# A Perceiver block on one core: the probabilities are turned by a DMA block exchange and VectorE's 32x32 transposes in place of TensorE's transposes

## What is computed

```python
def _L0_xattn_ref(query, key):            # query (1, 256, 2048), key (1, 25088, 2048)
    a = jnp.einsum('bqd,bkd->bqk', query, key)
    e = jax.nn.softmax(a, axis=-1)
    c = jnp.einsum('bqk,bkd->bqd', e, key)
    return c
...
    x = x + _L0_xattn_ref(_layernorm(x, axis=-1), ctx_4096)
    x = x + _L0_attn_ref(_layernorm(x, axis=-1), L0_attn_Wq, L0_attn_bq, L0_attn_Wk, L0_attn_bk, L0_attn_Wv, L0_attn_bv)
    x = x + _L0_ffn_ref(_layernorm(x, axis=-1), L0_ffn_W_base, L0_ffn_b_base, L0_ffn_W_gate, L0_ffn_A, L0_ffn_B)
```

## Time and profile before

| | us |
|---|---|
| median of 3 runs | 2488.42 |
| lowest and highest of them | 2483.71, 2494.42 |
| the profiled execution | 2496.61 |
| its span, from first to last instruction | 2494.9 |
| PE busy in it | 2443.1 (98%) |
| DVE, ACT and POOL busy | 1963.5 (79%), 1098.1 (44%), 1416.6 (57%) |
| mean clock granted to TensorE | 0.995 of full |

### The profile page before, as it was taken

How to read it: one execution, slowest core, us unless ns; L and a number is a source line. 1 busy time by engine, 2 the same in 40 slices (tenths; PEclk the granted TensorE clock), 3 DMA queues, 4 the chain that set the end, 5 groups by cost and what they waited for, 6 DMA issues and landing times.

```text
span 2494.9 us, 36102 instructions
## 1 busy us (share of the span) xinstructions
PE 2443.1 (98%) x11446; PEld 2011.2 (81%) x11446; DVE 1963.5 (79%) x2702; ACT 1098.1 (44%) x1577; POOL 1416.6 (57%) x1056
## 2 busy tenths in 40 slices
PE   6999999999999999999999999999999999999799
PEld 5888888888888888888888888888888888868577
DVE  8888888888878888888888888888878888674356
ACT  4444444444444444444444444444444444443443
POOL 2766666666666555566565565555656656552341
PEclk9999999999999999999999999999999999999899
DMA  9988888788888988888988888888898888878533
GB/s 237 255 213 229 219 207 231 207 232 217 205 231 217 224 216 217 211 220 204 230 215 201 220 218 218 216 212 220 206 228 210 208 218 218 214 158 156 130 121 100
DMA packets 421367, 518.22 MB, mean 208 GB/s; under 512 B 54470, under 2 KB 296134, under 8 KB 418504
## 3 DMA queue, kind: packets, MB, share of 16 engines
q1 hardware_dynamic: 411336, 475.66, 78.1%
q0 software_dynamic: 9984, 41.95, 5.1%
HBM read 488.71 MB, written 28.84 MB: 207 GB/s over the span
## 4 chain that ended last, share of the span: by engine, by line
PE 93%; SPq 3%; DMA 2%; DVE 1%; ACT 0%; issue 0%; ACTq 0%; DVEq 0%
PE ps L1457 30%; PE ps L1459 30%; PE ps L1458 30%; PE ps L1466 2%; SPq L439 1%; DMA q_t<-qk_dram 1%; SPq L567 1%; DMA quart<-in_ctx_dram 1%; PE ps L1686 0%; PE ps L1632 0%; PE ps L1759 0%; PE ps L1485 0%; DVE acc L1203 0%; DMA qk_dram<-q_nat 0%; SPq L432 0%
## 5 line engine op out<-in xcount | busy, mean ns | idle before, releaser
L618 POOL TENSOR_TENSOR nat_lo<-raw,nat_hi 128x512 fp32r<-128x512 f32 x784 | 1171.0, 1523 | 862.3 <-ACT nat_hi L778 830.2
L1082 DVE TENSOR_TENSOR ch_lo<-tr,ch_hi 128x512 fp32r<-128x512 f32 x784 | 762.2, 972 | 296.9 <-ACT ch_hi L767 293.2
L767 ACT CAST ch_hi<-tr 128x512 fp32r<-128x512 f32 x784 | 481.1, 621 | 796.9 <-PE ps L1459 776.9
L1457 PE MATMUL ps<-ch_hi,xt_hi 128*128 128x512 f32 x1696 | 673.1, 397 | 9.9 <-DVE ch_lo L1082 6.4
L1459 PE MATMUL ps<-ch_hi,xt_lo 128*128 128x512 f32 x1696 | 662.9, 391 | 0.0
L1458 PE MATMUL ps<-ch_lo,xt_hi 128*128 128x512 f32 x1696 | 662.2, 390 | 0.0
L1457 PE MATMUL ps<-nat_hi,pt_hi 128*128 128x512 f32 x1568 | 610.3, 389 | 1.6 <-DVE pt_lo L1023 1.6
L1459 PE MATMUL ps<-nat_hi,pt_lo 128*128 128x512 f32 x1568 | 610.3, 389 | 0.0
L1458 PE MATMUL ps<-nat_lo,pt_hi 128*128 128x512 f32 x1568 | 610.0, 389 | 0.0
L1078 DVE STREAM_TRANSPOSE tr<-quart 128x512 f32<-128x512 f32 x784 | 547.6, 699 | 2.1 <-DMA quart<-in_ctx_dram 2.1
L778 ACT CAST nat_hi<-raw 128x2048 fp32r<-128x2048 f32 x196 | 374.4, 1910 | 206.7 <-PE ps L1459 184.0
(11 more groups left out here) (200 smaller groups left out, 1397.8 us busy)
## 6 DMA issues: line engine op xcount, KB each, us to landing
quart<-in_ctx_dram SPq DMA_DIRECT2D x392, 512.0 KB, 8.4
raw<-in_ctx_dram SPq DMA_DIRECT2D x196, 1024.0 KB, 8.2
wq_in<-in_L_attn_Wq_dram POOLq DMA_DIRECT2D x16, 1024.0 KB, 6.4
win<-in_L_ffn_W_base_dram SPq DMA_DIRECT2D x64, 256.0 KB, 6.8
tr<-wt_dram POOLq DMA_DIRECT2D x64, 256.0 KB, 3.2
wt_dram<-stage SPq DMA_DIRECT2D x32, 256.0 KB, 5.5
wt_dram<-stage_b SPq DMA_DIRECT2D x32, 256.0 KB, 10.3
wq_dram<-wq_out POOLq DMA_DIRECT2D x16, 256.0 KB, 2.3
```

The source lines that it names most:

```text
L618: last = pool.tensor_tensor(nat_lo[:, j, t], raw[:, j % 2, t], nat_hi[:, j, t].bitcast(F32), ALU.subtract)
L767: act.copy(ch_hi[:, c % RING_CH, :], tr[:, c % RING_TR, :]).then_inc(chunk_hi, 1)
L1082: dve.tensor_tensor(ch_lo[:, c % RING_CH, :], tr[:, c % RING_TR, :], ch_hi[:, c % RING_CH, :].bitcast(F32), ALU.subtract).then_inc(chunk_s ...
L1457: pe.matmul(out_, a_hi, b_hi, start=start, stop=False)
```

## The change

The probabilities no longer go through TensorE, in the 47 turns for which `by_dma` holds (turns 2 to 48: not the first, not the second, not the end). Instead

- ACT writes `probs` with the keys of a tile in another order (the 32-key groups that belong to one partition quarter side by side),
- SP copies the four 128-column blocks of a query tile to the four partition quarters of a new tile `quads`, four DMAs of 64 KB for each tile (runs of 512 bytes), 8 for a turn, ahead of the next loads,
- DVE turns `quads` by 32x32 blocks back into `probs` (two instructions of 128x512 for a turn, `turn_probs`, which write every fourth element),
- `pt_hi` and `pt_lo` are then made out of `probs` in SBUF, not out of PSUM.

Pieces 0 and 1 of the sum stand one chunk later on PE, with them the first `nat_hi` piece on ACT and the first two updates of `acc` on DVE. On DVE the transposition of chunk c+3 now stands behind the work on the probabilities. `quads` takes the room of `b_nat`, so all 8 experts' loads stand in the last turn.

```diff
+        quads = put(at_b, "quads", [P, TT, QR, P])
...
+                self.by_dma = not (self.first or self.second or self.over)
...
-        PIECE_AFTER = {5: 0, 7: 1, 9: 2, 11: 3, 13: 4, 15: 5}
+        PIECE_AFTER = {6: 0, 8: 1, 9: 2, 11: 3, 13: 4, 15: 5}
...
+            def move_probs(turn, q):
+
+                sp.wait_ge(probs_ready, turn.times(TT, q + 1 - TT))
+                for b in range(QR):
+                    sp.dma_start(quads[b * SQ:(b + 1) * SQ, q], probs[:, q, b * P:(b + 1) * P]).then_inc(probs_moved[q], 16)
+
             def next_block(turn, m=None):
 
                 step = turn.step if m is not None else None
+                if turn.by_dma:
+                    for q in range(TT):
+                        move_probs(turn, q)
...
             next_block(REST[0], LAST_M)
-            for e in range(EXPERTS // 2):
-                load_expert(e)
...
+            for q in range(TT):
+                move_probs(REST[1], q)
             sp.wait_ge(chunk_transposed, DC * (NB - 1) + CH)
...
             sp.dma_start(x_nat[:], x_dram).then_inc(x_again, 16)
-            for e in range(EXPERTS // 2, EXPERTS):
+            sp.wait_ge(lo_drained, G_PT + TT * (NB - 1))
+            for e in range(EXPERTS):
                 load_expert(e)
...
             def softmax(turn, q):
...
-                act.activation(probs[:, q, :], ps[:, SCORE_BANK + TT * new + q, :], ACT.Exp,
+                to, of = probs[:, q, :], ps[:, SCORE_BANK + TT * new + q, :]
+                if turn.by_dma:
+                    to = to.rearrange("p (b t j) -> p t b j", b=QR, t=KT)
+                    of = of.rearrange("p (t b j) -> p t b j", b=QR, t=KT)
+                act.activation(to, of, ACT.Exp,
...
             def probs_group(turn, q):
-                hi_group(turn.times(TT, G_PT + q - TT), q, pt_hi[:, q], bank4(q))
+                if turn.by_dma:
+                    act.wait_ge(out_ready, turn.times(8, 6 + q + 1 - 16))
+                    hi_group(turn.times(TT, G_PT + q - TT), q, pt_hi[:, q], probs[:, q].rearrange("p (t m) -> p t m", t=KT))
...
-            ROWS = {11: 0, 15: 1}
+            ROWS = {12: 0, 15: 1}
...
+            def turn_probs(turn, q):
+
+                dve.wait_ge(probs_moved[q], turn.times(16 * QR, -16 * QR))
+                dve.transpose(probs[:, q].rearrange("p (t i a) -> p t a i", t=KT, a=QR),
+                              quads[:, q].rearrange("p a (t j) -> p t a j", t=KT)).then_inc(group_done, 1)
...
-            ADD_AFTER = {9: 0, 11: 1, 13: 2, 15: 3, 17: 4}
+            ADD_AFTER = {10: 0, 12: 1, 13: 2, 15: 3, 17: 4}
...
-                if v == 0:
+                if turn.by_dma and v < TT:
+                    pe.wait_ge(lo_drained, turn.times(TT, G_PT - 1 + v))
+                elif v == 0:
                     pe.wait_ge(lo_drained, turn.times(TT, G_PT))
...
-                    if c == (3 if turn.second else 1) and not turn.first:
+                    if c == 3 and turn.second:
                         for q in range(TT):
                             probs_group(turn, q)
```

19 lines of the change are left out of this document (13 added, 6 removed).

## The result

The changed kernel takes **2499.86 us** (median of 20 runs, 2486.88 to 2507.69), the kernel before 2490.46 us beside it (20 runs, 2483.71 to 2508.47). I had forecast 2460 us (2447 to 2487) and given "the same" a chance of 0.22. The profiled execution of the changed kernel is 2496.28 us, its span 2494.7, where the one before had 2496.61 and 2494.9: the two traces are as long as each other to 0.3 us, and can be laid side by side.

What follows compares the result with a forecast made beforehand. PE was taken as the bound, its transposes worth 41.8 us; 2496.6 - 41.8 + 3 (`win` turns) + 5 (turn 17) + 5 (last turn) = 2467.8 us, and the same 28.8 us off the median gave 2460 us, range 2447 to 2487.

Steps and rivals of the forecast that it cites:

- the same: Whole run: a change under 0.5% (12.4 us), neither below 2476.0 nor above 2500.9 us; chance 0.22.
- What bounds the kernel, and the 41.8 us: PE in 47 turns: back-to-back matmuls plus eight transposes a turn; removing these saves 47 x 0.89 = 41.8 us.
- DVE's list: DVE's steps in a turn: chunk 8 ready at T+18.0 to T+18.7, wanted at T+19.04, margin 0.3 to 1.0 us.
- the first rival: DVE's strided transposes cost much more: at 1.35 us each 2484 us (chance 0.08), at 1.75 us 2532 us (0.10).
- T: The time in a turn when PE starts chunk 0, from which the prediction counts microseconds.
- `win` ahead of the moves: 15 odd turns, 19 to 47: moves queue behind `win`, second tile 0 to 0.9 us late; 0.2 us a turn, +3 us.
- 15 x 2: Upper bound of the loss in the 15 turns with `win` ahead, 2 us a turn; lower bound 0.
- about 0.7: Margin in us that the second tile's lateness was set against in turns with `win` ahead.
- The second rival: Turns with `win` ahead: moves land 2 to 3 us late, 15 x 2 = +30, 2487 us, no change; chance 0.10.
- Turn 17: `win` waits for a store, moves come after it, there about T+12.5, 3.6 us late; +5 us once (3 to 8).
- The last turn: Eight experts' loads instead of four delay `raw` piece 2 and then PE at the end; +5 us (3 to 9).
- From the profiled run to the median: End of the sum: profiled run 8.2 us above the median of 2488.42, so the same 28.8 us off the median, 2459.6.

Runs made afterwards that it cites:

- experiment 1: The changed kernel with the four loads of `win` issued behind the eight moves of the same turn: 2468.35 us, ratio 0.9901.
- experiment 2: The changed kernel without the moves, DVE turning `probs` itself into `quads` (probabilities at wrong places): 2458.64 us, ratio 0.989.
- experiment 10: Kernel with `win` behind the moves, turns 2 and 48 over TensorE, experts' loads as before, plus dense writes of the turned transposes: 2452.01 us, ratio 0.9838.
- experiment 4: The changed kernel with the turned transposes writing densely, leaving out the interleaving of the keys: 2484.66 us, ratio 0.9966.

## Why the prediction failed, by its steps

- **What bounds the kernel, and the 41.8 us: right.** PE's turn without transposes was put at 43.53 us; it is 43.4 to 43.5 in 28 turns. With 47 turns the gain is 42.5 us, as reckoned.
- **DVE's list: right, by some luck.** I had the turned transposes at 0.70 us each; they are 1.08, so what the first rival names exists, but at 1.08 us and not at the 1.35 or 1.75 of its two cases. The steps behind them went somewhat faster than the 0.65 I took (most of them 0.57 to 0.63 in turn 19 of experiment 1), and chunk 8 was still ready at T+18.2, within my T+18.0 to T+18.7; the margin held (experiments 1, 2, 10).
- **`win` ahead of the moves: this is the step that failed. 3 us reckoned, 27 measured**, near the end of the bounds that I had set myself ("15 x 2"). I had the second tile at T+8.6 to T+9.8; it came at T+11.1 in turn 25. First, I took SP's 0.46 us for an issue from loads out of DRAM and let them begin at T-0.2; a move takes 0.60 us to issue, and behind `win` they begin at T+0.45, so the last is 1.4 us later. Second, I let the DMA engines be done with everything by T+7.6 to T+8.8; they stay full until past T+11, with `raw`, `win` and, behind the moves, the next quarters, and a move lands 5.7 to 8.0 us after its issue. My row of a full DMA at T+5 to T+6 said that there was a backlog, and I added one microsecond for the landing. Third, 0.77 us of dearer transposes had used a part of the "about 0.7" of slack against which I counted the lateness (with dense writes the loss is 19 us, experiment 4). The second rival (late moves, 2487 us, chance 0.10) described this mechanism and its size in these turns. With 2 us a turn in place of 0.2 the sum would have come to 2487, inside my range; turn 2 and the last step below carried the result beyond it.
- **What a wait costs:** I priced a stall at its length. Behind the waits of 2.33 us and more the clock was on its lower level for some microseconds, which the sum had nowhere; it is nearly 8 us of the loss.
- **Turn 17: right.** 5 us reckoned, 6.7 measured, for the reason given; 2.5 of it are slower matmuls behind the wait.
- **Turn 2: missing.** The sum treated it as one of 47 like turns, and it cost 7 us. I had read one late turn of the trace and none of the first.
- **The last turn: right where it was reckoned** (5.0 us at the second norm); it does not show in the length of the end (317.9 us against 318.7), which scatters by more than that.
- **From the profiled run to the median:** the sum, set right, is 2496.6 - 42.5 + 27 + 6.7 + 7 + 2 - 0.4 = 2496.4, against 2496.3 measured (the 0.4 is what lies ahead of turn 2 and behind turn 48). I then took off the 8.2 us by which the profiled run before lay above the median; the changed kernel's profiled run lies 3.6 us below its own median instead. One execution is not its kernel's median, and I had only one: before, it has the longest end of five with the same code there. Of the 40.3 us between forecast and result, 28.5 are thus the sum's and 11.8 this step's.

## What to carry to other kernels

A small transfer that an engine waits for should be priced by what the DMA engines still have to do when it is issued, on all queues, and not by its own bytes: here 64 KB landed in 2.6 us with `win` behind, in 4.3 us with 0.5 MB of it ahead and in 5.9 to 7.2 us with 1 MB ahead, and reordering the issues turned a loss of 0.3% into a gain of 1%. When a step leaves PE for a chain of other engines, its worst turns decide: look at each kind of turn (first, last, with side work), and add the lower clock behind each wait of some microseconds.

## What the runs showed of the hardware

- The 32x32 transpose on DVE of 128x512 fp32 takes 1082 ns when it writes every fourth element and 692 ns when it writes densely.
- An issue on SP takes 0.60 us for a move within SBUF, and 0.46 us for a load of `win`.
- Moves on SP's queue landed 6.0 to 6.8 us after their issue (medians of 15 turns) while ACT's queue carried 1 MB, and 5.9 to 7.2 us behind that 1 MB in their own queue: a queue of one's own did not change the landing.
- PE's granted clock went from 1.00 to 0.56 to 0.59 behind a wait of 3.98 us, to 0.59 behind one of 2.33 us, and stayed at 1.00 behind waits of 1.28 and 1.64 us, on an otherwise busy engine.
- A DVE subtraction of 128x512 that reads both operands from SBUF takes 0.66 to 0.69 us when POOL rests and took 1.57 us while POOL subtracted; with one operand out of PSUM it took 0.65 to 0.69 us in all 98 cases, POOL working or not.
